# A recurrence beside cross-attention on one core: fp32 probabilities as the stationary side of the PV product

## What is computed

```python
for l in range(4):                                  # sLSTM layers, 4 chains of 256 steps, 4 heads of 32
    x = x + slstm_layer(ln(x), ...)                 # scan over time; then per head (y - mean) * rsqrt(var) * gnw
    x = x + ffn(ln(x), ff_up[l], ff_down[l])        # GELU gate, 168 wide
scores = einsum('bqhd,bkhd->bhqk', q, k) * 64**-0.5 # 16 heads of 64, 6404 keys
out = einsum('bhqk,bkhd->bqhd', softmax(scores), v).reshape(...) @ Wo + bo
x = layernorm(x + out)
x = layernorm(x + top1_expert(x))                   # relu(x @ W1[e] + b1[e]) @ W2[e] + b2[e]
```

## Time and profile before

| | |
|---|---|
| runs, median of 3 | 4696.32 us (4688.74 to 4704.13) |
| the profiled execution's own time | 4716.16 us |
| its span | 4714.4 us |
| busy share | PE 84%, PEld 45%, DVE 78%, ACT 60%, POOL 22% |
| granted PE clock, mean over the span | 0.849 |
| recurrence with `ByHead` work | 123 to 929 us |
| recurrence with units | from 930 us; scores from about 1111 to 3301 us |
| tail, from the first score to the last product | 3399 to 4470 us |

### The profile page before, as it was taken

The page is one execution under the profiler, slowest core; times in us unless marked ns, Lnnn a source line. Parts: engine busy times, 40 slices in busy tenths (PEclk is TensorE's granted clock), DMA queues, the critical chain, the costliest instruction groups (busy, mean ns, idle before and its releaser), DMA issues. The chain is left out here.

```text
span 4714.4 us, 105294 instructions
## 1 busy us (share of the span) xinstructions
PE 3969.0 (84%) x38240; PEld 2143.3 (45%) x38240; DVE 3658.0 (78%) x15825; ACT 2850.1 (60%) x9049; POOL 1046.6 (22%) x1207
## 2 busy tenths in 40 slices
PE   4767777648999999999999999999588988898759
PEld 2333343334545445445454454544255555555436
DVE  4787888778888888887888888886678888887541
ACT  2555555535666666666666666667177777777712
POOL 1000000000000000000000000000288878888700
PEclk7555555557999999999999999999599999999969
DMA  2222222100000000000000000000312221222020
GB/s 62 66 70 70 68 70 70 60 3 3 2 4 4 2 4 2 3 4 2 3 2 3 3 2 3 2 2 3 93 39 71 73 73 42 67 72 58 3 57 5
DMA packets 97822, 146.85 MB, mean 31 GB/s; under 512 B 14077, under 2 KB 90549, under 8 KB 92150
## 3 DMA queue, kind: packets, MB, share of 16 engines
q1 hardware_dynamic: 97302, 140.13, 10.7%
HBM read 82.32 MB, written 56.56 MB: 29 GB/s over the span
## 5 line engine op out<-in xcount | busy, mean ns | idle before, releaser
L1270 PEld LDWEIGHTS G<-st,rec_w 128*128 128x128 f16 x19456 | 609.9, 100 | 894.7 <-DVE st L1430 854.6
L1664 POOL TENSOR_TENSOR plt<-pft,pht 128x512 f16<-128x512 f32 x765 | 875.2, 1169 | 244.2 <-DVE pht L1891 163.8
L1270 PE MATMUL G<-st,rec_w 128*128 128x1 f16 x19456 | 684.3, 165 | 286.9 <-DVE st L1430 268.8
L1222 PE MATMUL OA<-pf,vals 128*97 128x512 f32 (+1 forms) x1632 | 855.3, 605 | 0.7
L1166 ACT ACTIVATE st<-hb 32x16 f16<-32x16 f32 x1216 | 259.0, 213 | 704.0 <-DVE hb L1425 703.3
L267 DVE TENSOR_REDUCE mx<-MT 128x1 f32<-128x512 f32 (+1 forms) x832 | 520.9, 661 | 96.0 <-PE MT L1710 92.2
L1659 ACT ACTIVATE pft<-ST,ln_prob 128x512 f32<-128x512 f32 (+1 forms) x816 | 541.0, 687 | 64.1 <-PE ST L1732 63.5
L267 DVE TENSOR_REDUCE mx<-MB 128x1 f32<-128x512 f32 (+1 forms) x832 | 537.4, 660 | 48.2 <-PE MB L259 33.5
L1146 ACT ACTIVATE pf<-SC,ln_prob 128x512 f32<-128x512 f32 (+1 forms) x816 | 560.7, 687 | 20.5
L1657 ACT ACTIVATE pht<-ST,ln_prob 128x512 f16<-128x512 f32 x510 | 350.9, 688 | 264.4 <-PE ST L1732 259.0
L1157 ACT ACTIVATE tf<-G 32x16 f32<-32x16 f32 x1216 | 213.0, 175 | 366.3 <-PE G L1270 338.0
(11 more groups left out here) (321 smaller groups left out, 7484.2 us busy)
## 6 DMA issues: line engine op xcount, KB each, us to landing
vc<-scr_v SPq DMA_DIRECT2D x16, 1644.8 KB, 15.9
kc<-scr_k SPq DMA_DIRECT2D x32, 816.0 KB, 13.1
scr_v<-v_hl SPq DMA_DIRECT2D x24, 1032.0 KB, 5.6
scr_k<-k_hl SPq DMA_DIRECT2D x192, 128.0 KB, 1.7
k<-scr_k SPq DMA_DIRECT2D x16, 816.0 KB, 6.7
w<-in_L_ffn_W SPq DMA_DIRECT2D x16, 256.0 KB, 5.8
xin<-x SPq DMA_DIRECT2D x38, 48.0 KB, 1.8
scr_v<-v_hl SPq DMA_DIRECT2D x2, 774.0 KB, 5.7
```

Of the source, the lines that this page charges most:

```text
L1222: pe.matmul(OA[0:at.DC + 1, :], at.vals[0:rows, i, :], pf[0:rows, tile % 2, :], start=(i == 0), stop=(i == KT - 1)).then_inc(pv_done, 1)
L1270: mm = pe.matmul(g[:, t, c:c + 1], rec_w[:, c, :], st[:, c:c + 1], start=False, stop=(c == C - 1), skip_group_check=True)
L1664: return eng.tensor_tensor(pl[0:k, t % NP_, :], pf[0:k, t % NP_, :], ph[0:k, t % NP_, :], ALU.subtract)
```

## The change

In the recurrence's units the probabilities become the stationary side, once per head (`pe_values`): four fp32 matmuls of 97 moving columns. `OA` then holds query by feature. ACT keeps it, the denominator is a column of `o_sb`, PE turns the four heads (`pe_flip`) at step 2 after the unit, ACT copies the turned heads in two halves, PE projects at step 4, and DVE adds two heads in each of two steps. `pe_den` is gone.

In the tail `pht`, `plt`, their casts, second exps and subtractions are gone, and POOL has no part in the loop. The values lie as one fp32 copy. Per tile there are four fp32 matmuls of 65 moving columns with `pft` stationary. `OT`'s two banks alternate by head, and `keep_sums` is one copy.

The recurrence's heads are turned and centered by PE, sixteen fp32 matmuls of 32 rows, 32 stationary and 32 moving columns in steps 0 and 1 of a chunk, with the matrix `center`. DVE's four transposes, sum and subtraction go, and all that follows in the chunk moves up by about two steps. The gates take eight steps, 24 to 31, two cells in each.

In the first ten chunks keys and values have places of their own (11 and 11 in a chunk). Values are copied once by ACT to fp32, from the banks `MB`, and have no low part.

```diff
+def pe_values(pe, at, bank, probs, rows, j, last):
+    W = at.DC + 1
     for i in range(at.HEADS_A_UNIT):
-        mm = pe.matmul(bank[:, i:i + 1], at.o_sb[:, i * P:(i + 1) * P], at.pick_den[:, :], start=True, stop=True)
+        mm = pe.matmul(bank[:, i * W:(i + 1) * W], probs[0:rows, i * P:(i + 1) * P], at.vals[0:rows, j, :],
+                       start=(j == 0 and i == 0), stop=last, skip_group_check=True)
     return mm
+def pe_flip(pe, at, bank):
+    for i in range(at.HEADS_A_UNIT):
+        mm = pe.transpose(bank[0:at.DC, i * P:(i + 1) * P], at.o_sb[:, i, 0:at.DC], at.identa[:, :])
+    return mm
...
-        self.out = {start[u] + period: u for u in range(units - 1)}
+        self.flip = {start[u] + period + 2: u for u in range(units - 1)}
+        self.out = {start[u] + period + 4: u for u in range(units - 1)}
...
-    PLACES = (0, 1, 2, 3, 4, 5, 7, 8, 11, 12, 13, 14, 15, 18, 19, 20, 21, 25, 28, 30, 31)
+    KEY_PLACES = (2, 5, 6, 13, 16, 18, 19, 23, 27, 29, 31)
+    VALUE_PLACES = (3, 4, 9, 10, 12, 17, 21, 22, 25, 28, 30)
...
+        def pe_heads(pe, old, layers):
+            for l in layers:
+                for h in range(H):
+                    mm = pe.matmul(TP[l * CH:(l + 1) * CH, h * Q:(h + 1) * Q], old[:, 0:CH, l * H + h], center[:, :],
+                                   start=True, stop=True)
+            return mm
...
+                        if t == 0:
+                            pe_heads(pe, hb[(p + 1) % 2], range(0, L // 2))
+                        if t == 1:
+                            pe_heads(pe, hb[(p + 1) % 2], range(L // 2, L)).then_inc(B["yc"], 1)
...
-                            pair, third = divmod(t - T_GATES, 3)
-                            pe_gates(pe, new, k, pair, range(3 * third, min(3 * third + 3, 2 * L)))
+                            pair, quarter = divmod(t - T_GATES, 4)
+                            pe_gates(pe, new, k, pair, range(2 * quarter, 2 * quarter + 2))
...
-                        pe.matmul(OA[0:at.DC + 1, :], at.vals[0:rows, i, :], pf[0:rows, tile % 2, :], start=(i == 0),
-                                  stop=(i == KT - 1)).then_inc(pv_done, 1)
+                        pe_values(pe, at, OA, pf[:, tile % 2, :], rows, i, i == KT - 1).then_inc(pv_done, 1)
...
-                    if not hi_by_vector(t):
-                        s.activation(ph[0:k, t % NP_, :], SC[t % NS][0:k, :], ACT.Exp, scale=1.0 / at.S_SCALE,
-                                     bias=at.ln_prob[0:k, 0:1])
...
                     for i in range(NB):
-                        if j == 0 and g and i % 2 == 0:
-                            pe.wait_ge(o_free, 2 * g - 1 + i // 2)
-                        pe.matmul(OA[i // 2][:, (i % 2) * 256:(i % 2) * 256 + VC], ph[0:k, t % NP_, i * P:(i + 1) * P],
-                                  vc[0:k, g % 2, j, :], start=(j == 0 and i % 2 == 0), stop=False, skip_group_check=True)
+                        mm = pe.matmul(OA[g % 2][:, i * VC:(i + 1) * VC], pf[0:k, t % NP_, i * P:(i + 1) * P],
+                                       vc[0:k, g % 2, j, :], start=(j == 0 and i == 0), stop=(j == KT - 1),
+                                       skip_group_check=True)
+                    mm.then_inc(pv_done, 1)
                     if t + NS < TOTAL:
                         scores(t + NS)
...
-                    for i in range(NB):
-                        mm = pe.matmul(OA[i // 2][:, (i % 2) * 256:(i % 2) * 256 + DHEAD + 1], pl[0:k, t % NP_, i * P:(i + 1) * P],
-                                       vc[0:k, g % 2, j, 0:DHEAD + 1], start=False, stop=(j == KT - 1), skip_group_check=True)
-                    mm.then_inc(pv_done, 1)
...
-        vector_load = [0.4, 0.4, 0.4, 0.4, 0.6, 0.3, 0.6, 0.9, 0, 0.1, 0.4, 0.6, 0.7, 0.7, 0.35, 0.7, 0.1, 0.5, 0.35, 0.32,
-                       0.5, 0.6, 0.4, 1.2, 1.2, 0.6, 0.6, 0.5, 0.15, 0.15, 0.15, 0.3]
+        vector_load = [0.15, 0.15, 0, 0.3, 0.6, 0.9, 0, 0.1, 0.4, 0.6, 0.7, 0.7, 0.35, 0.7, 0.1, 0.4, 0.35, 0.16, 0.5, 0.2,
+                       0.4, 1.2, 1.2, 0.6, 0.5, 0.5, 0.5, 0.4, 0.15, 0.1, 0.1, 0.3]
```

339 lines of the change are left out of this document (146 added, 193 removed).

## The result

| | before | after |
|---|---|---|
| median of the runs (beside each other, 4 and 4) | 4694.93 us (4688.74 to 4704.13) | 4988.97 us (4982.69 to 5014.3) |
| ratio, 95% interval | | 1.0635 (1.0592 to 1.0677) |
| profiled execution, span | 4716.16, 4714.4 us | 5014.3, 5012.2 us |
| mean granted clock | 0.849 | 0.840 |

The change costs 294 us in the medians and 298 us between the two profiled spans. Both profiled executions above are on the long side, 21 and 25 us over their medians.

A forecast was written before the change was run, and what follows sets the result against it. PE was busy for 84% of the span, with unit steps ended by DVE or PE. Terms -55 - 15 + 175 + 150 + 10 on 4716 gave 4981 us profiled, 20 less as median: 4960 us (4850 to 5150).

The forecast's parts named there:

- The fp32 product's pace: Units and tail: loading 128 stationary fp32 columns sets about 0.11 us a record; product 0.86 us in units, 0.83 in tail.
- The tail: Tail: PE alone is late, 1.26 us a tile without a maximum, +175 us; clock there +10 us.
- The units: Recurrence's units: product's time unchanged at 0.86 us, small parts -55 us, slow steps after clock falls +150 us.
- The clock: Units: ten more slow steps after each of twelve falls, 120 steps at 1.25 us, +150 us.
- The three small parts: Units: the end of a unit, the gates and the heads, together -55 us.
- The end of a unit: Units: turns and projection in two steps, DVE's work in halves, -2 us for each of 15 units, -30 us (0 to -50).
- The gates: Recurrence chunks: two cells instead of three save 0.2 us in four steps a chunk, -10 us (+10 to -20).
- The heads: Chunk steps with heads' matmuls: DVE loses work, PE gains 16 matmuls at 0.45 us a step, -15 us (-40 to +30).
- The first ten chunks: First ten chunks: 102 value subtractions go, mostly off the path, and gates shrink beside key or value pieces, -15 us (0 to -35).
- The clock as now: Rival, whole program: the granted clock behaves as before the change, 4800 us, chance 0.27.
- Hidden loads: Rival, tail's product: fp32 stationary loads are hidden and a record costs its moving columns only, 4400 us, chance 0.06.
- A clock that stays low for most of the recurrence: Rival, units: 80% of the unit steps run at 1.2 GHz, 5630 us, chance 0.10.

The follow-up runs named there:

- the run with one step: The mixed version with a unit's end as in the kernel before, denominators, projection and all four DVE heads in one step: 4680.21 us, ratio 0.9966.
- the mixed version: The changed kernel with the tail, values and units' product of the kernel before, and heads on PE with the layer innermost: 4660.82 us, ratio 0.9924.

## Why the prediction held

The forecast was 4960 us, the result 4989 us, inside the forecast's own range. What carried it, the fp32 product's pace and with it the larger part of the tail's loss, was right. That the total is off by 29 us only is also luck: between the profiled executions the tail came out 78 us above its terms, and the units 29 us and the first ten chunks 15 us below theirs. By its steps:

**The fp32 product's pace: right, and shown.** 0.83 us was taken for the tail and 0.84 measured, 0.86 taken for the units and 0.86 measured. The run with 33 columns shows that the moving columns don't set it, and the loads in the traces, 191 ns in fp32 against 99 ns in fp16, point to the load of the stationary side. The count of four passes alone, which the prediction takes from the Trainium skill, page "FP8 and Floating Point Precision", would be 0.44 us and is ruled out for the tail; the measurement decides. On that load the Trainium skill, "TensorE: Matmul & The Clock Gate", section "Weight-path perf modes — Fast Weight Load (FWL) and DoubleRow", says that the fast load of weights is not for FP32. With that the trace agrees: four fp16 matmuls of 65 columns took 0.12 us before, four fp32 ones take 0.84 us.

**The tail: +185 forecast, +263 measured.** At 2.4 GHz the tail is 200 us longer where I had 175: a tile takes 1.29 us, not 1.26, and 816 times 0.03 us is 24 us of the 25. The step that failed is the tail's clock. I had +10 us and reasoned only from the head's starts, where the double bank helps. The cost was 62 us in the profiled execution, with 138 us at 0.50 at the tail's start, and 25 us in four other versions with the same tail. After its fall at the recurrence's end the clock came back to 1.00 after 99 us in all six versions with the tail of before, after 99 us too where long matmuls stood ahead of the new tail, after 157 to 160 us in five with the new tail and nothing ahead (one of them with 33 columns), and after 235 us in the changed kernel; the tail's products begin 95 to 99 us after that fall. The short falls later in the tail of before, of 3.4 us and 7 us, are gone with the new tail.

**The units: +95 forecast, +66 measured, as a sum of two errors.**
- *The clock*, +150 us: the direction is shown, and the size was too large. With the product of before, the stage has 181 us less at 0.50 and is 83 us shorter. By 4.3 us a step these are some 42 slow steps, not 120, and each costs 1.7 us more than a step at 1.00 (4.26 against 2.58), not 1.25: I had priced a step with the product and at most one maximum, and many steps carry a second maximum, gates or norms as well. Where they lie was wrong as well: I put ten steps behind each of twelve falls at a unit's end. In the profiled execution the seven falls at a unit's end lasted 3 to 24 us, much as before, and half of the time at 0.50 was in two falls of 64.9 us in the middle of a unit.
- *The three small parts*, -55 us together: with the product of before in the units the stage took 17 us less than in the kernel before (2354.7 against 2372.0). The next three points divide this.
- *The end of a unit*, -30 us: 19 us, shown by the run with one step. My reason was the shorter steps; by the time at 0.50 in the two profiles most of it is the clock, which fell less often. The units of the mixed version with heads on DVE differ from those before only in this end, and that program is 14 us below the kernel before (4682.87 against 4696.77 us), with first ten chunks 5 us longer, so the size holds there too.
- *The gates*, -10 us: 26 us in all, 17 of them in the units. I counted 0.2 us for the cell that goes, and not that PE ends the last steps of a chunk: in the kernel before, PE waited for nothing ahead of the recurrence's matmuls in any of a chunk's steps 27 to 31.
- *The heads*, -15 us (-40 to +30): this step failed. As the change has them they cost some 24 us more than in the better order, and in that order nothing is gained or lost by themselves. I had taken 0.45 us a step, a quarter of the load of 128 columns. It was 0.82 us, with neighbours on the same output partitions, and 0.36 us on different ones.
- In the profiles the mixed version's units are 47 us shorter than before, and end, gates and heads explain about 32. The other 15 us are near the 20 us by which the profiled execution of the kernel before lies above its median (mean clock 0.849, where the runs beside the others had 0.850 to 0.855).

**The first ten chunks: -15 forecast, -30 measured.** 27 us of it are the values' low part, in the version with the tail of before. Beside heads on DVE and gates in six steps the same low part is 16 us (810.4 against 794.5 us), so it depends on what stands beside it. I had argued that DVE's 160 us of idle time would cover most of the 69 us; a quarter to two fifths were on the path.

**The rivals.** The clock as now (4800 us) is out: it was not kept, in the tail either, although PE was busy in all of the 64.9 us and all of the 137 us shown above. Hidden loads (4400 us) are out by 0.84 us for four products of 65 columns, and by the 33 columns. A clock that stays low for most of the recurrence (5630 us) didn't come in the recurrence, but it did in the tail of the run with 33 columns, 5556 us. The changed tail, with 65 columns, kept 1.00 once it had it; how near it is to the other behaviour no run shows.

**What the sum of the runs shows.** From 4989 us, the product of before in the units takes 95 us off (some of it at the tail's start), the heads' order 24, and the tail of before with the values' low part 210 (4870 to 4661). That leaves the mixed version 36 us below the kernel before; taken back singly, the gates' eight steps are 26 us of it and the unit's end in several steps 19 us.

**Open.** Why a fall in the middle of a unit lasted 64.9 us at the same step of the same unit in three versions and 6.8 us in a fourth, is not known. In the changed kernel the other fall of 64.9 us is at the same step of a unit and of a chunk, eight units earlier. The steps before that place went differently in each, and no run holds them equal. Whether four long matmuls at a unit's start keep the clock is open too, since executions of the same units differ as much. It was also not tried whether a tail that makes its scores and fp32 products in another order would keep the clock from the start.

## What to carry to other kernels

Price an fp32 matmul by its stationary side first: with 128 stationary columns it cost 0.10 to 0.11 us a record and 0.20 to 0.22 us a matmul here, whether 33, 65 or 97 columns moved, so that turning the product to move fewer columns saved nothing (0.86 us either way), and against fp16 parts, whose loads took half as long, it lost. Before a step is made of many loads and short streams, look at the granted clock by stage, not at PE's busy share: PE was busy all the time in stretches at either clock, and sixteen long matmuls that compute nothing made the tail behind them 25 to 62 us shorter. Where the clock falls and rises within a program, one profiled execution is one draw: compare its time and mean clock with those of the other executions before a difference of stages is read from it. When a change loses, test its small parts alone: here they were worth 36 us, and the large idea hid that.

## What the runs showed of the hardware

- In the tail of fp32 products with 128 stationary columns, PE's records, scores and maxima included, followed each other at 7.3 to 7.5 a us at a granted clock of 1.00 and at 3.8 a us at 0.50, with 65 and with 33 moving columns alike.
- A load of 128 stationary columns took 191 ns in fp32 and 99 ns in fp16 at 1.00, and one of a single fp32 column 83 ns; in fp32 it was 191 ns with 65 and with 33 moving columns.
- With 33 columns in place of 65, in one execution, the granted clock was 0.50 for 1363 of 1899 us, with PE busy in all of them; stretches of 218.5 us at 0.50 and 122.9 us at 1.00 came by turns, four times.
- Sixteen records of fp32 matmuls of 32x32 took 0.82 us with the same output partitions for neighbours and 0.36 us with different ones.
- Time at 0.50 in the units cost 0.39 to 0.43 us per us, less than the 0.50 that work of PE alone at half the pace would cost: DVE, which ends some of the steps, is still waited for.
- Four executions of one program took 4890.76 to 4991.07 us, with mean granted clocks of 0.865 to 0.841; four with the product of before in the units took 4893.1 to 4894.58 us, all at 0.862 or 0.863.
